# A decoder layer on one NeuronCore: feed-forward and scan in halves of 256 tokens, softplus polynomial evaluated by its factors

## The reference, cut to what matters

```python
# 1 causal attention, 16 query heads of 32, 2 key/value heads, on layernorm(x)
# 2 a selective scan whose input is ctx (256 features) and whose gate is layernorm(x)
u  = silu(conv1d(ctx @ in_proj, 4 taps) + conv_b)          # 512 channels
dt = softplus(dt_proj(x_proj(u)[:16]) + dt_b)
for n in range(16):                                        # 16 states per channel
    s[n, t] = s[n, t-1] * exp(dt[t] * A[n]) + dt[t] * u[t] * B[n, t]
y  = sum(s[n, t] * C[n, t] for n) + D * u ;  y *= silu(layernorm(x))
# 3 feed-forward, 1408 wide, with the low-rank adapters of the best 2 of 8 experts per token
g, v = xf @ Wg.T, xf @ Wu.T
base = silu(g) * v @ Wd.T
for e in chosen: h = silu(g + g_lora[e]) * (v + u_lora[e]); acc += w[e] * (h @ Ad[e].T @ Bd[e].T)
```

## Time and profile before

| | us |
|---|---|
| three runs, median (lowest to highest) | 1651.23 (1647.77 to 1653.64) |
| the profiled execution | 1649.75 |
| its span, first to last instruction | 1647.9 |
| TensorE busy (matmuls) | 1406.0 |
| VectorE busy | 1218.4 |
| ScalarE busy | 604.9 |
| GpSimd busy | 111.9 |

### The profile page before, as it was taken

The page is one execution under the profiler, slowest core; times in us unless marked ns, Lnnn a source line. Parts: engine busy times, 40 slices in busy tenths (PEclk is TensorE's granted clock), DMA queues, the critical chain, the costliest instruction groups (busy, mean ns, idle before and its releaser), DMA issues.

```text
span 1647.9 us, 16148 instructions
## 1 busy us (share of the span) xinstructions
PE 1406.0 (85%) x5768; PEld 685.0 (42%) x5768; DVE 1218.4 (74%) x1411; ACT 604.9 (37%) x1436; POOL 111.9 (7%) x116
## 2 busy tenths in 40 slices
PE   5756767999888799899889699899879788799999
PEld 2333433443333354444334255444334345454434
DVE  4899996589989766759998865759998967623330
ACT  5165553323223584232232376242333267211110
POOL 0000001001100000000110000100210000100000
PEclk8855558999999699899999779899999869789999
DMA  4167761123666631112656822012556741101112
GB/s 185 39 147 153 154 141 27 44 66 108 143 141 166 166 66 26 39 50 78 159 128 159 196 68 52 26 37 84 124 131 152 173 135 27 26 13 64 48 32 83
DMA packets 53278, 158.81 MB, mean 96 GB/s; under 512 B 5072, under 2 KB 10704, under 8 KB 44752
## 3 DMA queue, kind: packets, MB, share of 16 engines
q0 software_dynamic: 9216, 67.11, 19.8%
q1 hardware_dynamic: 25664, 54.23, 9.9%
q10 hardware_dynamic: 18320, 36.45, 8.6%
HBM read 86.20 MB, written 4.46 MB: 55 GB/s over the span
## 4 chain that ended last, share of the span: by engine, by line
DVE 30%; issue 30%; PE 29%; DMA 6%; ACT 4%; POOL 2%; DVEq 0%; ACTq 0%; POOLq 0%
DVE state L1091 11%; DMA y_sb<-state 5%; PE ps_a L894 5%; DVE state L1086 4%; PE ps_a L974 4%; PE ps_a L820 3%; DVE state L1096 3%; PE ps_b L834 3%; PE ps_w L873 3%; PE ps_a L906 3%; POOL rstd L477 2%; PE ps_b L914 2%; PE ps_w L782 2%; ACT r L625 2%; DVE neg_max L1126 2%
## 5 line engine op out<-in xcount | busy, mean ns | idle before, releaser
L894 PE MATMUL ps_a<-xt,w_sb 128*128 128x512 f32 x704 | 319.2, 607 | 0.0
L1091 DVE TENSOR_TENSOR_SCAN state<-decay,state 128x2048 f32<-128x2048 f32 x64 | 282.8, 4418 | 5.3 <-ACT decay L583 0.5
L677 ACT ACTIVATE r<-ps_a 128x512 f32<-128x512 f32 x132 | 78.6, 596 | 380.6 <-PE ps_a L906 202.8
L894 PEld LDWEIGHTS ps_a<-xt,w_sb 128*128 128x128 f32 x704 | 138.1, 197 | 174.9 <-issue 174.9
L820 PE MATMUL ps_a<-r 32*128 32x512 f32 (+3 forms) x512 | 140.4, 634 | 81.7 <-ACT r L625 55.2
L906 PE MATMUL ps_a<-r,wb_sb 128*128 128x512 f32 x352 | 177.1, 628 | 35.9 <-DVE r L1267 33.7
L583 ACT ACTIVATE decay<-dt_sb,decay_rate 128x511 f32<-128x511 f32 x256 | 162.9, 712 | 104.9 <-DVE state L1096 72.2
L1260 DVE SCALAR_TENSOR_TENSOR r<-r,ps_a 128x512 f32<-128x512 f32 x132 | 89.9, 681 | 146.3 <-ACT r L677 146.3
L625 ACT ACTIVATE r<-ps_a,neg_max 128x128 f32<-128x128 f32 (+3 forms) x256 | 133.6, 534 | 116.6 <-DVE neg_max L1126 116.1
L974 PE MATMUL ps_a<-wd_sb,r 128*128 128x512 f32 x352 | 162.4, 613 | 0.0
L1086 DVE TENSOR_TENSOR state<-du_sb,bc_sb 128x2048 f32<-128x2048 f32 x64 | 146.3, 2286 | 4.7 <-DMA y_sb<-state 4.6
(11 more groups left out here) (120 smaller groups left out, 1475.7 us busy)
## 6 DMA issues: line engine op xcount, KB each, us to landing
y_sb<-state POOLq DMA_DIRECT2D x64, 1024.0 KB, 9.7
bc_sb<-bc_rows ACTq DMA_DIRECT2D x64, 512.0 KB, 5.1
w_sb<-in_w_tiles SPq DMA_DIRECT2D x44, 512.0 KB, 3.7
wd_sb<-in_w_down SPq DMA_DIRECT2D x44, 256.0 KB, 3.5
wb_sb<-in_w_adapt SPq DMA_DIRECT2D x44, 128.0 KB, 2.1
xa<-in_x SPq DMA_DIRECT2D x4, 1024.0 KB, 5.2
out_x<-xb SPq DMA_DIRECT2D x16, 256.0 KB, 7.0
xn_att<-in_ctx_t SPq DMA_DIRECT2D x4, 512.0 KB, 6.1
```

What stands on the lines that cost most here:

```text
L894: mm = nc.tensor.matmul(ps_a[:, 2 * (f % 2) + half, :], w_sb[:, slot, at + k * P:at + (k + 1) * P], xt[:, k, :], start=(k == 0), stop=Fals ...
L1091: nc.vector.tensor_tensor_scan(flat, decay[:, n % 2, :, :].rearrange("p j l -> p (j l)"), flat, 0.0, ALU.mult, ALU.add).then_inc(scan_chai ...
```

## The change

The feed-forward and the scan are done in **units** of 256 tokens (`HALVES = 2`, `UNITS = 8`), attention stays whole. A unit's 11 tiles go in six pairs (`FP`), the weights through four slots (`WS`, two before), and they are loaded once for each unit. The order of a batch is now attention, z stage, feed-forward of the first half (the **even unit**), feed-forward of the second half (the **odd unit**).

```diff
+HALVES = 2
+HL = L // HALVES
+FP = (FT + 1) // 2
+WS = 4
 EVAL = [(0, 0)]
-for _f in range(FT):
-    EVAL += [(_f, 1)] + [(_f + 1, 0)] * (_f + 1 < FT) + [(_f, 2)]
+for _p in range(FP):
+    EVAL += [(_p, 1)] + [(_p + 1, 0)] * (_p + 1 < FP) + [(_p, 2)]
```

The places of the scan's pieces. `("s", b, s)` is an attention step, `("z", b, k)` the z stage and the even unit's head, `("e", u, e)` and `("d", u, f)` gate and down stage of a unit:

```diff
+Z_COUNTS = [1, 1, 1, 1, 1, 1, 2, 1, 2, 1, 2]
+for _u in range(UNITS):
+    _b, _h = divmod(_u, HALVES)
+    _pieces = [(kind, n, _u) for kind, n in STATE_PIECES]
+    if _h == 0:
+        _pieces = [("poly", k, _u) for k in range(NPOLY)] + _pieces
+        if _b == 0:
+            _where = list(zip([("d", -1, f) for f in range(FT)], [5, 5] + spread_over(3, FT - 2)))
+        else:
+            _where = list(zip([("e", _u - 1, e) for e in range(6, EVALS)], spread_over(NPOLY, EVALS - 6)))
+            _where += list(zip([("d", _u - 1, f) for f in range(FT)], spread_over(20, FT)))
+        _rest = len(_pieces) - sum(count for _, count in _where)
+        _where += list(zip([("s", _b, s) for s in range(STEPS - 1)], spread_over(_rest, STEPS - 1)))
+    else:
+        _where = list(zip([("z", _b, k) for k in range(ZSLOTS)], Z_COUNTS))
+        _where += list(zip([("e", _u - 1, e) for e in range(1, EVALS)], spread_over(26, EVALS - 1)))
+        _rest = len(_pieces) - sum(count for _, count in _where)
+        _where += list(zip([("d", _u - 1, f) for f in range(5)], spread_over(_rest, 5)))
+    place(_pieces, _where)
```

The state works on rows of 257 elements; the last column of the first half is carried to the second. The product goes to a buffer of its own, and it is now `out` that waits for the sum two half states back:

```diff
 mul:
+    if h > 0:
+        nc.vector.tensor_copy(state[:, slot, :, 0:1], carry[:, n, :].unsqueeze(2))
-    tt(state[:, n % 2, :, :], du_sb[:], row, ALU.mult)
+    tt(inner, du_sb[:, :, h * HL:(h + 1) * HL], row, ALU.mult)
 out:
+    if h == 0:
+        nc.vector.tensor_copy(carry[:, n, :].unsqueeze(2), state[:, slot, :, HL:SW])
+    if g >= 2:
+        dve.wait_ge(y_added, 16 * (g - 1))
-    tt(state[:, n % 2, :, :], state[:, n % 2, :, :], row, ALU.mult)
+    tt(prod[:, slot, :, :], inner, row, ALU.mult)
```

The polynomial (degree 9) is multiplied out of one real root and four conjugate pairs. ScalarE squares, VectorE multiplies, each half of the channels in turn:

```diff
+            def square(b, k):
+                if k >= 2:
+                    act.wait_ge(poly_chain, b * NPOLY + k)
+                tiles = slice(k % 2 * JT // 2, (k % 2 + 1) * JT // 2)
+                nc.scalar.activation(square_sb[:, tiles, :], exp_v[:, tiles, :], ACT.Square,
+                                     bias=cst[:, C_ROOT + k // 2:C_ROOT + k // 2 + 1]).then_inc(square_ready, 1)
...
+                if k == 0:
+                    stt(du_sb[:].rearrange("p j l -> p (j l)"), flat, -POLY_LINE, flat, ALU.add, ALU.mult)
+                elif k <= QUADS:
+                    dve.wait_ge(square_ready, b * QUADS + k)
+                    stt(part, square_sb[:, tiles, :].rearrange("p j l -> p (j l)"), POLY_PAIRS[(k - 1) // 2][1], part,
+                        ALU.add, ALU.mult).then_inc(poly_chain, 1)
```

In a unit TensorE works on pairs of tiles, with 256 columns, gate and up in one bank:

```diff
-for half, at in ((0, WG), (1, WU)):
-    for k in range(KT):
-        mm = nc.tensor.matmul(ps_a[:, 2 * (f % 2) + half, :], w_sb[...], xt[:, k, :], ...)
+for w, f in enumerate(pair_tiles(p)):
+    for half, at in ((0, WG), (1, WU)):
+        for k in range(KT):
+            mm = nc.tensor.matmul(ps_a[:, pair_bank(p) + w, half * HL:(half + 1) * HL], w_sb[...], xt2[:, k, :], ...)
```

More of the change, by code:

```diff
@@ L64 @@
 EVALS = len(EVAL)
 STEPS = MT * NT * 2
[L67 to L77, removed]
+X_SLOT = 2
+DT_SLOTS = (4, 5)
+NORM_SLOTS = (9, 11, 13, 15)
 PV_AT = 5
 OUT_AT = (STEPS - 1, STEPS + 1, STEPS + 2, STEPS + 3)
[L80 to L90, removed]
@@ L93, in plan @@
[L93 to L109, removed]
+ZSLOTS = 11
@@ L112, in spread_over, with pair_tiles @@
+OUT_BANK = (3, 1)
+def pair_tiles(p):
+    return range(2 * p, min(2 * p + 2, FT))
 def spread_over(total, places):
     return [(k + 1) * total // places - k * total // places for k in range(places)]
[L116 to L125, removed]
@@ new lines, with place, between @@
+KEYS = timeline()
+SLOT = {key: {"dve": [], "bc": [], "decay": [], "add": [], "square": []} for key in KEYS}
+KEY_AT = {key: i for i, key in enumerate(KEYS)}
+PIECE_AT = {}
+def place(pieces, counts):
+    k = 0
+    for key, count in counts:
+        for piece in pieces[k:k + count]:
+            SLOT[key]["dve"].append(piece)
+            PIECE_AT[piece] = KEY_AT[key]
+        k += count
+    assert k == len(pieces), (k, len(pieces))
+def between(free, used):
+    for i in range(free + 1, used):
+        kind, _, s = KEYS[i]
+        if kind != "e" or EVAL[s][1] == 1:
+            return i
+    return min(free + 1, used)
@@ new lines @@
+STATE_PIECES = [(kind, n) for n in range(NS) for kind in ("mul", "run", "out")]
+Z_COUNTS = [1, 1, 1, 1, 1, 1, 2, 1, 2, 1, 2]
[17 more added lines that the diff above has]
+    place(_pieces, _where)
@@ new lines @@
+for _g in range(UNITS * NS):
+    _u, _n = divmod(_g, NS)
+    _v, _m = divmod(_g - 2, NS)
+    _free = PIECE_AT["out", _m, _v] if _g >= 2 else -1
+    if _n < 2 and _u % HALVES == 0:
+        _free = max(_free, PIECE_AT["poly", NPOLY - 5, _u])
+    SLOT[KEYS[between(_free, PIECE_AT["mul", _n, _u])]]["bc"].append(_g)
+    _free = PIECE_AT["run", _m, _v] if _g >= 2 else -1
+    if _n < 2 and _u % HALVES == 0:
+        _free = max(_free, PIECE_AT["poly", NPOLY - 1, _u])
+    SLOT[KEYS[between(_free, PIECE_AT["run", _n, _u])]]["decay"].append(_g)
+    SLOT[KEYS[PIECE_AT["out", _n, _u]]]["add"].append(_g)
@@ L131, in projections @@
+for _b in range(BATCH):
+    for _k in range(2, QUADS):
+        _free, _used = PIECE_AT["poly", _k - 1, HALVES * _b], PIECE_AT["poly", _k + 1, HALVES * _b]
+        SLOT[KEYS[between(_free, _used)]]["square"].append((_b, _k))
 def projections(f):
@@ L157, in value_groups, with next_batch @@
     return [(s - PV_AT) // 2] if PV_AT <= s < PV_AT + STEPS - 3 and (s - PV_AT) % 2 == 0 else []
[L160 to L176, removed]
+def next_batch(u):
+    b, h = divmod(u, HALVES)
+    return b + 1 if h == HALVES - 1 and b + 1 < BATCH else None
@@ L448, in _, with store @@
+            def store(u):
+                b, h = divmod(u, HALVES)
+                for i in range(HT):
+                    sp.wait_ge(x3_ready, u * HT + i + 1)
+                    sp.dma_start(out[b].rearrange("(i p) d -> p i d", p=P)[:, h * HT + i, :], xb[:, h * HT + i, :])\
+                        .then_inc(stored, 16)
             load_ctx(0)
@@ new lines, in _ @@
+            for u in range(UNITS):
+                b, h = divmod(u, HALVES)
+                if h == 0 and b + 1 < BATCH:
+                    load_ctx(b + 1)
+                if next_batch(u) is not None:
+                    load_x(b + 1)
+                for f in range(WS, FT):
+                    load_w(u, f)
+                    load_wb(u, f)
+                for f in range(WS):
+                    load_wd(u, f)
+                if u + 1 < UNITS:
+                    for f in range(WS):
+                        load_w(u + 1, f)
+                        load_wb(u + 1, f)
+                for f in range(WS, FT):
+                    load_wd(u, f)
+                store(u)
@@ L1156, in attention @@
                     if s < STEPS:
-                        for piece in slots[ATT + s]["dve"]:
-                            scan_piece(b, piece)
+                        pieces(("s", b, s))
                     for g in value_groups(s):
```

1128 lines of the change are left out of this document (614 added, 514 removed).

## The result

The changed kernel took **1716.91 us**, the median of four runs (1713.29 to 1721.45), where the kernel before took 1652.43 beside it (four runs, 1647.77 to 1653.94): a ratio of 1.0397, 95% interval 1.0363 to 1.0430. It is 4% slower; I had forecast 1641, 0.6% faster, with 1690 as the high end.

A forecast was written before the change was run, and what follows sets the result against it. VectorE, unevenly loaded, alone bounds the first attention; later ones are a three-engine chain. Batch-wise terms -69.1, +7.6, +10.7, +14.1 and +27.0 sum to -9.7: span 1638.2, written as 1641 us, range 1600 to 1690.

The forecast's parts named there:

- Gate stages: Gate stages of a batch's two units: even 68 us, odd 70, together 138 for 151.9, -13.9 a batch.
- Down stages: Down stages of a batch's two units: even 26.5 us, odd 51.5, together 78 for 84.9, -6.9 a batch.
- the 5 that I named: Sign before the odd head's first transposes: TensorE idle for some 5 us.
- Later attentions: Attentions after the first, with 28 half pieces each: 85 us for 79.8, +5.2 a batch.
- attention is paced by pieces: Rival in attention: pieces raise a step from 2.65 to 3.0 us, three attentions 33 longer, 1674; chance 0.15.
- Heads: Start of each unit's feed-forward, now two per batch: 61.8 us for 40.5, +21.3 a batch.
- z stages: Stage after attention: six scan pieces, two in gaps, four lengthening it, gate 1.5 us shorter: +5.0 a batch.
- Last unit: Final odd unit, without VectorE work beside it: head 27 us, gate stage 61, down stage 26.
- Setup: Setup: polynomial 10 us shorter, but two squares precede it and the first `run` moves in: 81.4 to 76, -5.4.
- the unit prices: Costs per instruction: 128x1024 on VectorE 1.22 us, half scan 2.28, half-sum DMA 5.9, ScalarE decay about 0.45.
- half sums at nearly the price of whole ones: Rival in first attention, even units and down stages: half sums at 8.1 us each, giving 1689; chance 0.15.
- Weight loads: Rival on TensorE: loads no longer hidden under 256 columns, 1296 pairs at 0.11 us, +143, 1784; chance 0.05.

The follow-up runs named there:

- e3: Changed kernel with the same pieces per gate stage, but none between an evaluation and the one the base product waits for: 1666.2 us, ratio 1.0084.
- e5: Against e3, nine first-half state pieces moved from the odd down stage (20 to 11) into the odd gate stage: 1676.3 us, ratio 1.0154.
- e9: Against e3, five pieces moved from the odd down stage (20 to 15) into the odd gate stage, no slot over two: 1674.79 us, ratio 1.0150.
- e8: Against e3, six pieces moved from the odd down stage (20 to 14) to the later attentions (28 to 34): 1662.66 us, ratio 1.0083.
- e6: Against e3, nine pieces moved from each later attention (28 to 19) into the odd gate stage: 1679.05 us, ratio 1.0173.

## Why the prediction was wrong

The forecast's span was 1638.2 us, the profiled one 1719.3: 81 more. By its own steps, after minus forecast:

- **Gate stages: the step that failed**, 47 of the 81. The prediction said "-13.9 a batch, since the stalls behind 4.4 us scans go". They did not go: 151 to 152 us a steady batch, as before. I had added what each engine has and taken the larger (VectorE 65, TensorE 59), and let the pieces be halved without reading where the new table puts them. Even gates took 74 to 75 for 68, odd ones 77 for 70. e3 moved the pieces and nothing else, and the even ones came to 63.8 to 65.1, below my 68: the sum was possible, the placing prevented it. (That they came below is in part luck: VectorE was busy for 56 to 58 us there, where I had 65.) Of the odd ones' 7 us e3 gave back 1.4 to 3.4. e5 and e9 show the same kind of cost in the odd ones: pieces added there delay the evaluations by about two thirds of their length, so the largest engine is no bound when the others feed it one by one. That the rest of the odd ones' excess is this cost too was not tested.
- **Down stages**, +21. Odd ones 55.4 for 51.5: in all three TensorE waited 7.9 us for `finish`, which stood behind pieces; I had written "coupling" for it and not looked at what stands last in the queue. e5 shows 48.4 without it. Even ones 28.9 for 26.5: the last `out` ended at 759.2, 19 us into the stage as forecast (18.5), but its DMA was issued only at 762.73, when the one before had landed. Pieces came every 4.9 us there and a sum, to landing and the next issue, took up to 7.0. VectorE's gate with `y` waited 8.01 us for the last DMA:

```profile
758.01 1.22 DVE L1176 TENSOR_TENSOR area<-area,bc_sb 128x1024 f32<-128x1024 f32 x1
767.24 1.23 DVE L1255 SCALAR_TENSOR_TENSOR silu_z<-y_sb,silu_z 128x1024 f32<-128x1024 f32 x1 [8.01 <-DMA y_sb<-area]
```

  TensorE had work until 766.3 and waited 2.23 us before this odd head, for the 5 that I named (3.3 in the first batch, 2.2 in the next two, 5.9 in the last).
- **Later attentions**, 89 for 85, +12.7 in all; the first 111.4 for 106, with VectorE busy for 102.2 (92%, not the 95 that I had named as its sign). In the later ones TensorE was busy for 80 to 83 us, at 0.73 to 0.74, where I had carried over 73 at 0.80: I held its busy time fixed while I added waits beside it. The rival "attention is paced by pieces" (33 us more) had the sign: adding pieces costs (e8). What taking nine away gives (e6), which part is the clock and which the chain, stays open.
- **Heads**, +5: even ones 30.0 (30.5 forecast), odd ones 33.6 (31.3). **z stages** 9.6 less than forecast. **Last unit** 110.5 for 114. The heads were the largest cost of the change, 88 us (84 forecast), and this part was read rightly from the last batch's rows.
- **Setup**, 78.5 for 76. I had covered the squares by VectorE's multiplications. A square took 1.15 us (I took 1.0 to 1.4), but in the setup ScalarE moves other tiles first, and VectorE waited for one (timeline of VectorE, kernel after):

```profile
52.86 2.36 DVE L1127 SCALAR_TENSOR_TENSOR du_sb<-dt_sb,du_sb 128x1024 f32<-128x1024 f32 x2 [4.21 <-ACT dt_sb L613]
```

- **Right**: the unit prices but the decay's, VectorE's total (1221 us), and the passes: 32 of 256 columns in 7.07 us, 0.22 each.

The rivals: half sums at nearly the price of whole ones would have given 1689, nearest the result, but that is luck: its cause was not there. It wanted 8.1 us for a half sum with its issue; a landing took 5.5, the next issue came 0.5 to 0.8 after it in the even down stage, and in the first attention VectorE never waited for `y_sb`. The even down stages did feel the chain of sums. Weight loads stayed hidden: 32 of them at 200 ns would have nearly doubled those 7.07 us. The Trainium skill, page TensorE: Matmul & The Clock Gate, Part 3, has a load overlap a matmul in flight only on different row groups; here both used all 128 rows and the trace disagrees, now at 256 columns too.

My range ended at 1690 because each rival was priced alone. Coupling in the gate stages had no rival of its own on the slow side.

## What to carry to other kernels

When an in-order engine does filler work beside a chain, the table of the filler is part of the price: read, for each wait of the bounding engine, which instruction ends it and what the new order puts ahead of that one. 51 us hung on the places alone, with every instruction the same. When an edit changes the number of filler pieces, keep the others in their places before judging it: the same polynomial was worth +12 us and -8 us.
